# A four-layer graph network on one core: the second norm laid between the target tiles, roots and inverses by chunk, two centerings folded into weights

## The reference

```python
x = _layernorm(x + _L0(x, ...))   # GRU network: 2 rounds of messages
x = _layernorm(x + _L1(x, ...))   # relational network: 3 convolutions with mean per relation
x = _layernorm(x + _L2(x, ...))   # GCN
x = _layernorm(x + _L3(x, ...))   # edge-mean MLP

def _layernorm(x, axis=-1, eps=1e-05):
    m = jnp.mean(x, axis=axis, keepdims=True)
    v = jnp.var(x, axis=axis, keepdims=True)
    return (x - m) / jnp.sqrt(v + eps)

# _L2: deg = how often a node is a row; dinv = 1/sqrt(deg), or 0
msgs = (dinv[row] * dinv[col])[:, None] * x[col]
agg = segment_sum(msgs, row)
return agg @ W.T + b
# _L3
h = concatenate([x, rec_attr, sent_attr]) @ W1 + b1    # means of the attributes by row and by col
return leaky_relu(h, 0.01) @ W2 + b2
```

## Time and profile before

| | |
|---|---|
| time, median of 3 executions | 3008.59 us (2991.08 to 3008.98) |
| the profiled execution | 3015.57 us |
| its span in the trace | 3013.5 us, mean granted TensorE clock 0.91 of 2.4 GHz |
| PE busy | 2499.6 us (83%) |
| PE weight loads | 2213.7 us (73%) |
| DVE busy | 1822.8 us (60%) |
| ACT busy | 861.0 us (29%) |
| POOL busy | 1585.2 us (53%) |
| chain that ended last, by engine | PE 71%, issue 10%, DVE 7%, DMA 6% |

### The profile page before, as it was taken

How to read it: one execution, slowest core, us unless ns; L and a number is a source line. 1 busy time by engine, 2 the same in 40 slices (tenths; PEclk the granted TensorE clock), 3 DMA queues, 4 the chain that set the end, 5 groups by cost and what they waited for, 6 DMA issues and landing times.

```text
span 3013.5 us, 45749 instructions
## 1 busy us (share of the span) xinstructions
PE 2499.6 (83%) x15645; PEld 2213.7 (73%) x15645; DVE 1822.8 (60%) x6123; ACT 861.0 (29%) x1512; POOL 1585.2 (53%) x1706
## 2 busy tenths in 40 slices
PE   7587777888587999458999989989899887877899
PEld 3376665676477989248999988888888876767796
DVE  4565655566485877235876655778755554433585
ACT  2354544445353111113222221112211110333101
POOL 0666666663566665643566446666366664466200
PEclk9788888889799999759999999999999997888899
DMA  7311112111398665019899788777878762466792
GB/s 270 108 52 50 51 49 53 50 51 30 126 275 247 177 168 158 14 33 285 268 274 276 226 277 244 239 228 227 275 228 239 233 206 60 145 217 219 231 268 76
DMA packets 271661, 520.15 MB, mean 173 GB/s; under 512 B 62015, under 2 KB 115698, under 8 KB 270645
## 3 DMA queue, kind: packets, MB, share of 16 engines
q1 hardware_dynamic: 185197, 289.49, 30.6%
q0 software_dynamic: 86224, 227.59, 26.0%
HBM read 323.93 MB, written 192.99 MB: 172 GB/s over the span
## 4 chain that ended last, share of the span: by engine, by line
PE 71%; issue 10%; DVE 7%; DMA 6%; another core or an unknown queue 4%; ACT 2%; POOL 1%; SPq 0%; DVEq 0%; POOLq 0%; ACTq 0%
PE ps L996 21%; PE ps L968 11%; PE ps L849 8%; PE ps L1187 6%; PE ps L981 5%; PE ps L1212 4%; PE ps L835 4%; PE ps L843 4%; DMA rec<-chunks,idx 2%; DMA chunks<-xs 2%; PE ps L1037 1%; DVE shot L1923 1%; PE ps L1043 1%; DMA srow<-lanes_of_slots 1%
## 5 line engine op out<-in xcount | busy, mean ns | idle before, releaser
L695 POOL DMA_INDIRECT rec<-chunks,idx x596 | 588.5, 987 | 498.4 <-PE ps L996 182.1
L996 PE MATMUL ps<-dhot,rec 128*128 128x168 f32 x4768 | 762.0, 313 | 79.7 <-issue 39.0
L996 PEld LDWEIGHTS ps<-dhot,rec 128*128 128x128 f32 x4768 | 708.1, 194 | 108.2 <-issue 84.8
L1944 DVE TENSOR_SCALAR dhot<-iota,dcode 128x168 f32<-128x168 f32 x2384 | 583.5, 310 | 215.4 <-PE ps L996 97.1
L695 POOL DMA_INDIRECT msg<-messages,idx_buf x416 | 400.0, 962 | 312.4 <-issue 191.7
L968 PE MATMUL ps<-hrow,shot 126*128 126x128 f32 x4000 | 509.0, 282 | 61.9 <-DVE shot L1923 29.9
L968 PEld LDWEIGHTS ps<-hrow,shot 126*128 126x128 f32 x4000 | 489.8, 197 | 78.3 <-issue 56.4
L1315 ACT ACTIVATE xs<-ps 128x512 f32<-128x512 f32 x500 | 294.1, 597 | 755.9 <-PE ps L968 408.2
L704 POOL DMA_INDIRECT attributes<-w,rank_to x368 | 369.8, 1005 | 230.8 <-issue 124.2
L1923 DVE TENSOR_SCALAR shot<-srow,lane_no 126x512 f32<-126x512 uint8 x500 | 230.6, 486 | 111.3 <-PE ps L968 46.7
L849 PE MATMUL ps<-big,lane1h 128*128 128x300 f32 x832 | 231.1, 430 | 6.6 <-issue 6.2
(11 more groups left out here) (292 smaller groups left out, 2529.5 us busy)
## 6 DMA issues: line engine op xcount, KB each, us to landing
chunks<-xs SPq DMA_DIRECT2D x375, 256.0 KB
tmp<-inverse_counts SPq DMA_DIRECT2D x36, 1008.0 KB
chunks<-xs SPq DMA_DIRECT2D x125, 258.0 KB
srow<-lanes_of_slots SPq DMA_DIRECT2D x100, 320.0 KB
grec<-chunks SPq DMA_DIRECT2D x125, 256.0 KB
messages<-big SPq DMA_DIRECT2D x25, 504.0 KB
trow<-lanes_of_targets SPq DMA_DIRECT2D x30, 320.0 KB
rec<-chunks,idx POOLq DMA_INDIRECT x596
```

Of the source, the lines that this page charges most:

```text
L695: eng.indirect_dma_start(buf, None, table, bass.IndirectOffsetOnAxis(ap=index, axis=0)).then_inc(sem, 16)
L996: last = mm(ps[:, 4 + i % 2, (v % 3) * WT:(v % 3 + 1) * WT], rec[:, v % RS, j * P:(j + 1) * P], dhot[:, v % DS, j * WT:(j + 1) * WT], star ...
L1944: last = vec.tensor_scalar(dhot[:, v % DS, j * WT:(j + 1) * WT], iota[:, 0:WT], dcode[:, v, j:j + 1], None, ALU.is_equal)
```

## The change

- **Norm 1 among the target tiles.** A new function `stage1_steps()` gives one list of steps, in which PE, ACT and DVE each take their own part. Ahead of tile 0 stand chunk 0 (finish, center, spread of dinv, variance, norm), the finish, center, spread and variance of chunk 1, and unit 0 of the GCN rows. Chunk 1's norm follows tile 0. Chunks 2 to 6 follow at the tiles of NORM_AT (6, 22, 38, 54, 70), each in five parts two tiles apart, its unit of GCN rows three tiles after the last. The one-hots run THOT_AHEAD = 3 tiles ahead. The target degrees move from tile 20 to 86, the means from 40 to 92. Banks: 3 for centering, 4 for dinv, 5 for variances and the spread inverse, 6 and 7 for GCN rows. The copy of spread dinv moves from the DVE to ACT.
- **Roots and inverses by chunk** in all four norms.
- **Centerings of norms 2 and 3 folded into weights.** In layer two, at tiles 86 and 92, PE transposes the weights `gcn` and `w2` and multiplies them and their two biases by the centering matrix; ACT copies the results back. Norm 2 needs, with centred weights, `x` of norm 1 as it is (already centred), so no centering matmul, no `ln_keep`. `centered_square` reads `acc` and writes the square to `h`.
- **The tail interleaved.** Three variances and inverses of norm 2 ahead, the rest one per round; the last norm's spreads and applies go as LAST_NORM says.
- **One conditional block** for `general(2, 3, 4)`; that of `degrees()` is gone, its reduce stands ahead of the block.
- **Attributes.** Four groups, not five: 16 sends that stood after layer 4 now stand among layer one's tiles.
- Semaphores are renamed where one counts two things.

```diff
-DST_AT, MEAN_AT = 20, 40
-AT = {1: range(0, 12), 2: range(12, 28), 3: range(28, 39), 4: range(39, 50), 5: range(50, 52)}
+DST_AT, MEAN_AT = 86, 92
+NORM_AT = {2: 6, 3: 22, 4: 38, 5: 54, 6: 70}
+THOT_AHEAD = 3
+LAST_NORM = {NCH: (0, 1, 2), NCH + 1: (3, 4), NCH + 2: (5,), NCH + 3: (6,)}
+AT = {1: range(0, 14), 2: range(14, 30), 3: range(30, 41), 4: range(41, 52)}
...
+        def stage1_steps():
+
+            first = [("finish", 0), ("center", 0), ("spread", 0), ("finish", 1), ("variance", 0), ("center", 1), ("norm", 0),
+                     ("spread", 1), ("variance", 1), ("unit", 0)]
+            at = [(-1, i, kind, n) for i, (kind, n) in enumerate(first)] + [(1, 0, "norm", 1), (5, 0, "unit", 1)]
+            for c, v in NORM_AT.items():
+                at += [(v - 2, 0, "finish", c), (v, 1, "center", c), (v + 2, 2, "spread", c), (v + 4, 3, "variance", c),
+                       (v + 6, 3, "norm", c)]
+                at += [(v + 9, 4, "unit", u) for u in range(YU) if unit_chunk(u) == c]
+            at += [(DST_AT, 5, "degrees", 0)] + [(MEAN_AT + 8 * c, 6, "mean", c) for c in range(NCH)]
+            at += [(v, 9, "tile", v) for v in range(NW)]
+            return [(kind, n) for _, _, kind, n in sorted(at)]
...
                 if i % 2 == 0:
                     send_attrs(1, AT_FIRST[1] + i // 2)
+                if i % 8 == 1:
+                    send_attrs(1, AT_FIRST[1] + (NQ + 1) // 2 + 1 + i // 8)
...
             after(eng, "acc_evac", 4, NGRP)
-            for k in (2, 3, 4):
-                general(k)
-            for n in range(G * len(AT[GCN])):
-                send_attrs(GCN, n)
+            general(2, 3, 4)
...
+            def turn_weights():
+
+                eng.wait_ge(q("aside_kept"), NCH)
+                for i, name in enumerate(("gcn", "w2")):
+                    last = mm(ps[:, 3, i * P:(i + 1) * P], wt(name), wt("ident"), start=True, stop=True, is_transpose=True)
+                last.then_inc(q("aside_mm"), 1)
+
+            def center_weights():
+
+                eng.wait_ge(q("aside_kept"), NCH + 1)
+                for i, name in enumerate(("gcn", "w2")):
+                    mm(ps[:, 3, i * P:(i + 1) * P], wt(name), wt("center"), start=True, stop=True)
+                mm(ps[:, 3, 2 * P:2 * P + 2], wt("center"), bias[:, B_AT["gcn"]:B_AT["gcn"] + 2], start=True, stop=True)\
+                    .then_inc(q("aside_mm"), 1)
...
-            def ln_spread(r, c, bank_no):
-                after(eng, "ln_rstd", r, 1)
-                if c >= 2:
-                    after(eng, "ln_out", r, c - 1)
+            def ln_spread(r, c):
+                back = 1 if r == 1 else 2
+                after(eng, "ln_rstd", r, c + 1)
+                if c >= back:
+                    after(eng, "ln_out", r, c - back + 1)
...
             general(GCN)
-            for i in range(NCH + 1):
-                if i < NCH:
-
-                    after(eng, "ln_in", 2, min(i + 2, NCH))
-                    ln_center(2, i, 0 if i % 2 else 7)
-                if i >= 1:
-                    ln_var(2, i - 1, 1)
+            for c in range(3):
+                ln_var(2, c)
             for i in range(NCH + 4):
                 if i < NCH:
-                    ln_spread(2, i, 6 if i % 2 else 2)
+                    ln_spread(2, i)
+                if i + 3 < NCH:
+                    ln_var(2, i + 3)
...
                 if 3 <= i < NCH + 3:
-                    after(eng, "ln_in", 3, i - 2)
-                    ln_center(3, i - 3, 7 if i % 2 else 0)
-                if i >= 4:
-                    ln_var(3, i - 4, 1)
-            for c in range(NCH):
-                ln_spread(3, c, 6 if c % 2 else 2)
+                    ln_var(3, i - 3)
+                for c in LAST_NORM.get(i, ()):
+                    ln_spread(3, c)
```

647 lines of the change are left out of this document (358 added, 289 removed).

## The result

The changed kernel took 2958.40 us (median of 4 executions, 2939.71 to 2971.03); the kernel before, run beside it, 3004.35 us. The ratio is 0.9853, 95% interval 0.9818 to 0.9888: faster by 1.5%. The medians lie 46 us apart, where 36.5 were forecast. The profiled execution took 2971.03 us, its span is 2969.2 (before 3013.5, and the table of the profile), so the two traces differ by 44.3 us.

What follows compares the result with a forecast made beforehand. The prediction saw a serial handover, a target stage with no engine full, and a PE-bound tail. Terms -34.5 + 8 - 13.5 + 3.5 = -36.5 took 3008.59 to 2972.1 us; own range 2960 to 2985, wider 2947 to 2992.

Steps and rivals of the forecast that it cites:

- the small additions: Layers one to three: extra sends +1.5, layer two's weights +1, more inverses on the DVE +1; sum +3.5 us.
- The serial piece: Handover from the third relational layer to the target tiles, 2521 to 2579 us: blocks, then a norm phase by phase; forecast -34.5.
- Entry, 12.3 to 7.3 us: Conditional blocks after layer four: PE's pause falls from 12.3 to 7.3 us with one merged block.
- the same proportion: Entry: PE's pause shrinks as the DVE's blocks do, 12.3 x 2.92 / 4.89 = 7.3 us.
- an even third, 4.1: Entry, low end: PE's pause falls to 4.1 us; with full clock, the handover gains 42 us.
- is not what PE waits for: Entry: the DVE finishes chunk 0 by about 2528.6 us, before PE is ready at 2531.2.
- First chunk and a half: Handover: PE's norm work on chunk 0 and the front of chunk 1 takes 13.3 us before tile 0.
- must leave this place: Handover: 16 attribute sends on POOL must move, else the first put would stand behind them.
- Target stage, +8: Target tiles: about 18.5 us of added PE work, mostly covered by waits; +8 us, ends 0 and +33.
- Rivals 1, 2 and 4: Target stage: 1, nothing covered, +33, chance 0.15; 2, stage shorter, -19, 0.14; 4, ring locks, +103, 0.04.
- Tail, -13.5: After the GCN sums: no centerings left, PE stays the bound; end at 3000.0 against 3013.5 us, -13.5.
- The end given for this term (-9): Tail, smallest gain: the DVE in line, its three applies ahead of the last sum; -9 us.

Runs made afterwards that it cites:

- m1: Changed kernel plus one small product of constants on PE behind the conditional block, as a marker; executed once, handover 20.0 us, tail 48.0.
- m3: Changed kernel plus a marker product on PE, with three conditional blocks after layer four instead of one; executed once, handover 25.2 us, tail 46.2.
- b1: The kernel before, unedited, profiled a third time; executed once, handover 48.6 us, tail 56.5.
- p1: Changed kernel with the last 16 attribute sends back behind layer four, in five groups; ratio to the kernel before 0.9885.
- x2: Changed kernel with five constant products in the tail, layer four's last wait inside the block on PE and DVE, and 16 sends back behind layer four; ratio 0.9823.
- t1: Changed kernel with two products of constants on PE in the pause ahead of norm 2; ratio to the kernel before 0.9846.
- b0: The kernel before, unedited, profiled a second time; executed once, handover 56.4 us, stage 200.0, tail 56.4.
- a1: The changed kernel repeated without an edit; 2637.00 us, ratio to the kernel before 0.9842.
- t3: Changed kernel with two constant products in the pause ahead of norm 2 and three wide ones between its first variances; ratio to the kernel before 0.9853.
- the fourth group: Runs on one chip beside the kernel before, which takes 2679 us there; b1, a1 and x2 belong to it.

## Why the prediction was right, and where not

The direction and the mechanism held. The measured median, 2958.4 us, lies 13.7 under the forecast of 2972.1 and just outside the forecast's own range of 2960 to 2985, within the wider one (2947 to 2992); 4 us of it are that the kernel before came out at 3004.35 beside it and not at 3008.59. Of the four terms three are right in sign, two of them off in size; the fourth, the small additions, didn't show. The three large terms sum to -38.6 us where -40.0 was forecast, and that closeness has luck in it: the tail gave 5.1 us less, the stage and the handover 3.7 more. That the traces differ by 44.3 us and not 36.5 comes from the end of layer four (8.4 us off the forecast), which no edit explains, and 0.8 us in the GCN sums, less the 1.4 us of the three terms.

**The bound.** The serial piece was where the time went: s1, which puts norm 1 back ahead of the tiles, gives up 35 us, nearly all of the gain (some of it to its own worse order).

**Entry, 12.3 to 7.3 us.** Measured 6.5 (6.4 in m1), but by a wrong step: "I take the same proportion", that of the DVE, for PE. PE needs 4.8 us for one block and 8.2 more for the other two, the DVE 4.6 and 0.4. The low end of the range (an even third, 4.1) was nearer for PE. The sentence that the DVE "is not what PE waits for" is the one that failed: it counted 2.92 us for the DVE's block by the third block of the earlier trace rows, and the merged one costs 4.6, most of it in the 3.85 us of "issue". The two errors cancelled to 0.8 us. The Trainium skill ("Runtime: NRT & Kernel Launch", Instruction fetch mechanics) says that a taken branch out of the fetched window stalls on a fetch; that three merged into one stall once is what the prediction drew from it, and m1 and m3 agree for PE. A fetch itself is seen in no trace here.

**First chunk and a half, 13.3 us at the low clock.** Measured 13.3, at the low clock as assumed. Together with the entry the handover is 20.0, where tile 0 "at about 20" was forecast. Against b1, whose norm had its clock back early, the same 20.0 saves only 28.6 us.

**The sends "must leave this place".** Wrong for this kernel: p1 shows the first put 1.6 us clear of them. It becomes right as soon as tile 0 comes earlier (x2, +10 us).

**Target stage, +8.** Measured +5.1, then +3.5, +3.7 and +1.2 (m1, t1 and m3 against b0), +2.2 (a1 against b1), and 2.4 to 2.9 between s1 and two neighbours. Cover by PE's pauses is better than assumed: 1 to 5 of 18.5 us come through. POOL's wait for ACT in the stage, named as 55 us, is 80.3 - 33.5 = 46.8, as before the change (47.6). The piece of degree matmuls of the earlier trace rows was no model for pieces of one chunk. Rivals 1, 2 and 4 didn't come about; the clock of the stage went from 0.86 to 0.88 only.

**Tail, -13.5.** Measured -8.4 to -8.5 against before in three pairs, -10.2 in m3. The step that failed is costing the rounds and variances at the distances of the earlier trace rows, a full-clock stretch, all through. The earlier trace rows already had 0.91 for this stretch. The new tail was at 1.2 GHz for 13.6 us and lost 6.8 by it; the rest of the sum was 1.7 us too long, which hid part of it. t3, with the clock at 1.00 throughout and its added products taken off, gives 41.9 for the 42.9 forecast. The likely reason for the fall is that removing the centerings took away the wide products between the one-column variances of norm 2; t1 and t3 support this, with the limits said there. The end given for this term (-9) was missed by 0.6 us.

**Small additions, +3.5.** In the first pair layer four ended 4.9 us earlier instead. That isn't explained by an edit: beside b0 and b1 the kernels with the extra sends end layer four 2 us later on average (0.1, 1.1 and 5.1; 3.5 and -1.1). That fits +3.5 as well as it fits 0; the spread between executions is as large.

By the same terms measured in the fourth group: -28.6 for the handover (b1 being the execution with the early clock; -36.4 against b0), +2.2, -8.5, and layer one to four +3.5, in all -31.4 for spans that differ by 32.5. The medians there differ by 42.
